# A transformer block on one core: its early transfers relaid and put in another order

## The chip, the core and the metric

The kernel runs on one core of one Trainium2 chip. The metric is device time in microseconds (us) from start to end of one execution. The engines are called PE (TensorE), DVE (VectorE), ACT (ScalarE), POOL (GpSimd) and SP (SyncE, which here only issues DMAs). They run side by side, each through its own instructions in order, and wait for one another through semaphores. 16 DMA engines move data from HBM to the core's memory (SBUF).

## What is computed

`x` is 1024 tokens by 256. A conditioning vector `c` gives six modulation vectors (shift, scale and gate, for the attention part and for the feed-forward part). The block is:

```python
mod = (silu(c) @ wmod).reshape(1, 6, 1, 256)
sa, ca, ga, sb, cb, gb = (mod[:, i] for i in range(6))
ga = (2 * (ga >= 0) - 1) * maximum(abs(ga), 0.25)      # gb likewise
h = layernorm(x) * (1 + ca) + sa
x = x + ga * attention(h)      # 64 latents, compressed to 32, norm, q k v, rotary, causal softmax
h = layernorm(x) * (1 + cb) + sb
x = x + gb * ffn(h)            # 2048 hidden; gate, up and down weights in 4 bits with a scale per 32
```

## The kernel before, in words

Everything is resident in SBUF. The 1024 tokens are 8 tiles of 128, worked on in two halves of 4 tiles (h = 0, 1). The feed-forward weights come in 8 groups of 256 hidden units; ACT, DVE and POOL decode a group while PE multiplies with an earlier one. The order on each engine is written out by hand, and there is no scheduler. Each row of code is one instruction or a short run of them in that order.

The order of the transfers is the order in which SP issues them (L306 to L315): the first half of `x`, `consts` (an identity of 128x128 first, then two selection matrices, two masks and four columns), the columns of `wmod` for shift and scale of the attention part, the second half of `x`, the other four of the six vectors' columns of `wmod` (1024 KB), the rotary table `rope`, and then for each group g its `packed` bits and its `scales`. ACT issues four small ones beside them (L326 to L329: `c`, two packs of small attention weights of 168 and 20 KB, the output bias). Both queues feed the same 16 DMA engines. `scales` has 8 rows per group, each spread over 16 partitions.

The beginning runs as one chain through several engines:

- DVE takes the statistics of the first half of `x` (`stats1(0)`, L553 to L560, waits for `x_in[0]`). POOL adds two weights (L514, waits for `a64_in`) and then makes the reciprocal root (`rsqrt`, L501). DVE normalises (L570).
- PE first multiplies a tile of zeros 14 times (`stay_warm`, a helper that only keeps PE busy), then with the small weights (waits for `a64_in`, `wsum_ready`), 3 more times zeros, transposes the normalised half (`transpose1(0)`, L891, against the identity), makes shift and scale (`mod_columns`, waits for `wmod_in[0]`), and compresses (`project_c(0)`).
- Then PE waits for `wmod_in[1]` and makes the gate `ga` (`products(bank(GA_B, D), ...)`), multiplies zeros 4 times, and turns the compressed half around (`transpose_c(0)`, L930, waits for `chat_ready`, which DVE gives at L599). With that, DVE's `gamma_beta(0)`, PE's `project_qkv(0)`, DVE's `rotate(0)` (waits for `rope_in`) and PE's `stack_qk(0)` follow one from another.

Every small instruction of PE is recorded at L866, the helper `mm`. The lines on which the order of PE's beginning rests are these:

```python
            project_c(0)
            pe.wait_ge(wmod_in[1], 16)
            products(bank(GA_B, D), [(silu[:, k:k + 1].to_broadcast([P, P]), wmod_sb[:, k, GA * D:(GA + 1) * D])
                                   for k in range(KT)]).then_inc(ga_done, 1)
            stay_warm(3, 4)
            transpose_c(0)
```

Of the kernel before, what the change touches and what calls it, by code (L numbers as in the profile page):

```python
# [27 lines left out]
P = 128  # L28
T, D = 1024, 256
DLAT, DC = 64, 32  # L30
FF = 2048
TILES = T // P
HALF = 512
HT = HALF // P
# [15 lines left out]
C_ID, C_SELQ, C_SELK, C_MASK, C_MASKT, C_QM = 0, P, 2 * P, 3 * P, 4 * P, 5 * P  # L50
# [20 lines left out]
def build_block(nc, x, wmod, c_col, attn64, attn32, b_out, consts, rope, packed, scales, out):  # L71
    with ExitStack() as ctx:  # L72
# [13 lines left out]
        xres = sb("xres", [P, TILES, D])  # L86
        wmod_sb = sb("wmod_sb", [P, KT, 6 * D])
# [58 lines left out]
        wmod_flat = wmod_sb[:].rearrange("p k n -> p (k n)")  # L146
# [5 lines left out]
        ident = cst[:, C_ID:C_ID + P]  # L152

        x_in = [sem("x_in0"), sem("x_in1")]
        c_in, a64_in, a32_in, cst_in, bout_in, rope_in = sem("c_in"), sem("a64_in"), sem("a32_in"), sem("cst_in"), sem("bout_in"), sem("rope_in")
# [74 lines left out]
        x_d = x[0].rearrange("(i p) d -> p i d", p=P)  # L230
        out_d = out[0].rearrange("(i p) d -> p i d", p=P)
        wmod_d = wmod.rearrange("(k p) n -> p k n", p=P)
# [71 lines left out]
        @block.sync  # L304
        def _(sp):
            sp.dma_start(xres[:, 0:HT, :], x_d[:, 0:HT, :]).then_inc(x_in[0], 16)  # L306
            sp.dma_start(cst[:], consts).then_inc(cst_in, 16)
            sp.dma_start(wmod_sb[:, :, 0:2 * D], wmod_d[:, :, 0:2 * D]).then_inc(wmod_in[0], 16)
            sp.dma_start(xres[:, HT:, :], x_d[:, HT:, :]).then_inc(x_in[1], 16)
            sp.dma_start(wmod_sb[:, :, 2 * D:], wmod_d[:, :, 2 * D:]).then_inc(wmod_in[1], 16)  # L310
            sp.dma_start(rope_sb[:], rope).then_inc(rope_in, 16)
            for g in range(GROUPS):
                sp.dma_start(wbuf[:, g, 0, :].bitcast(I32), packed[g]).then_inc(bits_in[g], 16)

                sp.dma_start(wbuf[:, g, 1, :],  # L315
                             scales[g].unsqueeze(1).to_broadcast([P // REP, REP, WORDS])
                             ).then_inc(scale_in[g], 16)
# [223 lines left out]
        def _(dve):  # L541
# [81 lines left out]
            def split_qk(h):  # L623

                dst = (QS[0:QK, h, :], KS[0:QK, HALF * h:HALF * (h + 1)])
# [238 lines left out]
        def _(pe):  # L864
# [8 lines left out]

            def mod_columns(o, vec, paired):
                for k in range(KT):
                    base = vec * D + (k if paired else k * P)
                    step = 2 if paired else 1
                    for kt in range(KT):
                        last = mm(o[:, k:k + 1], wmod_sb[:, kt, base:base + step * (P - 1) + 1:step],
                                  silu[:, kt:kt + 1], kt == 0, kt == KT - 1)  # L880
                return last

            def transpose1(h):
                pe.wait_ge(cst_in, 16)
# [58 lines left out]
            def stack_qk(h):  # L943

                pe.wait_ge(prod_ready, h + 1)
# [117 lines left out]
            products(bank(GA_B, D), [(silu[:, k:k + 1].to_broadcast([P, P]), wmod_sb[:, k, GA * D:(GA + 1) * D])  # L1063
# [32 lines left out]
            products(bank(3, D), [(silu[:, k:k + 1].to_broadcast([P, P]), wmod_sb[:, k, GB * D:(GB + 1) * D])  # L1096
# [101 lines left out]
```

## Time and profile before

| what | value |
|---|---|
| time, median of 3 runs | 216.76 us (214.21 to 218.32) |
| time of the profiled execution | 217.49 us |
| its span, first to last instruction | 215.5 us |
| mean granted clock of PE | 0.949 |
| busy: PE, DVE, ACT, POOL | 198.3, 142.7, 90.8, 59.4 us |
| bytes read from HBM | 10.09 MB |
| SP waits, longest | 123.4 us for DVE, before it stores the first output |

The profile is of one execution. The span does not hold what lies around the first and the last instruction, about 2 us here. The granted clock is the share of full speed that the chip's throttle left to PE: 1.0 is 2.4 GHz, 0.5 is 1.2 GHz.

### The profile page before, as it was taken

How to read it: one execution, taken by the hardware profiler on the slowest of the kernel's cores; microseconds unless marked ns; L12 is line 12 of the kernel's file. 1: busy time of each engine (PE TensorE's matmuls, PEld its weight loads, DVE VectorE, ACT ScalarE, POOL GpSimd, SP SyncE). 2: the span in 40 equal slices, each digit the busy share in tenths (PEclk: the TensorE clock that was granted, in tenths of full speed). 3: DMA queues.
4: the chain of work that ended last, by engine and by line, in shares of the span. 5: the costliest groups of instructions: out<-in, count | busy, mean ns of one | idle time of the engine just before them, and what ended most of it. 6: DMA issues, size and time to landing. Idle time of an engine off the chain costs nothing. (4 is left out here: it accounts for less than half of the span.)

```text
span 215.5 us, 3087 instructions
## 1 busy us (share of the span) xinstructions
PE 198.3 (92%) x1064; PEld 159.3 (74%) x1064; DVE 142.7 (66%) x267; ACT 90.8 (42%) x151; POOL 59.4 (28%) x52
## 2 busy tenths in 40 slices
PE   7899998999769969989999999999899999999991
PEld 2496476574446848878898889887698889889891
DVE  0665995878799999999999844945832333323235
ACT  2011141642478526437535556354243542552420
POOL 4404043515152620200000000463342633624200
PEclk9885895599999999999999999999999999999998
DMA  5999675400000000000000000000200000000002
GB/s 177 324 349 235 193 230 196 171 4 3 0 0 2 0 0 3 2 0 0 3 0 0 3 0 0 0 0 5 97 2 0 0 0 0 3 0 0 0 0 97
DMA packets 5644, 11.30 MB, mean 52 GB/s; under 512 B 544, under 2 KB 2752, under 8 KB 5632
## 3 DMA queue, kind: packets, MB, share of 16 engines
q1 hardware_dynamic: 5216, 10.82, 16.0%
q10 hardware_dynamic: 416, 0.33, 0.6%
q8 instruction: 7, 0.11, 0.2%
q14 instruction: 5, 0.04, 0.1%
HBM read 10.09 MB, written 1.05 MB: 52 GB/s over the span
## 5 line engine op out<-in xcount | busy, mean ns | idle before, releaser
L866 PE MATMUL ps<-H,WS 128*128 128x512 f32 x384 | 94.7, 394 | 3.6 <-DVE wmod_sb L714 2.8
L866 PEld LDWEIGHTS ps<-H,WS 128*128 128x128 f32 x384 | 69.6, 188 | 18.9 <-DVE wmod_sb L714 4.3
L866 PEld LDWEIGHTS ps<-WS,IS 128*128 128x128 f32 x384 | 49.8, 191 | 3.8 <-issue 1.7
L866 PE MATMUL ps<-WS,IS 128*128 128x256 f32 x384 | 50.9, 283 | 1.1 <-DVE wmod_sb L714 0.9
L429 ACT ACTIVATE IS<-wmod_sb 128x512 fp32r<-128x512 f32 x32 | 20.3, 634 | 64.1 <-PE ps L866 41.0
L284 DVE TENSOR_TENSOR IS<-wmod_sb,IS 128x512 fp32r<-128x512 f32 x32 | 22.1, 690 | 26.6 <-ACT IS L429 25.0
L293 POOL TENSOR_TENSOR WS<-wbuf,WS 128x1024 fp32r<-128x1024 f32 x10 | 24.2, 2421 | 50.3 <-ACT WS L410 50.3
L714 DVE TENSOR_TENSOR wmod_sb<-ps,wmod_sb 128x512 f32<-128x512 f32 x32 | 22.0, 688 | 22.7 <-PE ps L866 20.7
L298 POOL TENSOR_TENSOR WS<-wbuf,WS 128x512 fp32r<-128x512 f32 x10 | 13.7, 1371 | 38.4 <-ACT WS L417 38.4
L423 ACT ACTIVATE wmod_sb<-ps 128x512 f32<-128x512 f32 x32 | 18.7, 586 | 6.2 <-PE ps L866 6.2
L866 PE MATMUL ps<-idle 128*128 128x512 bf16 x46 | 16.3, 502 | 1.3 <-POOL idle L487 1.3
L410 ACT ACTIVATE WS<-wbuf 128x1024 fp32r<-128x1024 f32 (+1 forms) x16 | 16.8, 1051 | 0.0
L501 POOL TENSOR_TENSOR rstd<-var,power 128x4 f32<-128x4 f32 x6 | 7.2, 1202 | 34.2 <-DVE var L560 27.2
L866 PEld LDWEIGHTS ps<-idle 128*128 128x128 bf16 x46 | 5.2, 122 | 8.5 <-issue 5.4
L866 PE MATMUL ps<-PH,VS 128*128 128x512 f32 (+3 forms) x24 | 8.9, 402 | 2.7 <-DVE PL L258 2.1
L696 DVE SCALAR_TENSOR_TENSOR wbuf<-dec_b,wbuf 128x768 f32<-128x768 f16 x8 | 10.9, 1366 | 0.1
L417 ACT ACTIVATE WS<-wbuf 128x512 fp32r<-128x512 f32 (+1 forms) x16 | 9.9, 618 | 0.0
L553 DVE BATCH_NORM_STATS2 stats<-xres 128x6 f32<-128x256 f32 x16 | 5.6, 415 | 5.0 <-DMA xres<-x 5.0
L401 ACT ACTIVATE dec_a<-wbuf 128x768 int32<-128x768 uint8 x8 | 6.7, 838 | 4.8 <-DMA wbuf<-packed 4.8
L687 DVE SCALAR_TENSOR_TENSOR dec_b<-dec_a,dec_b 128x768 int32<-128x768 int32 x8 | 8.3, 1042 | 0.1
L866 PEld LDWEIGHTS ps<-PH,VS 128*128 128x128 f32 x24 | 4.8, 206 | 4.4 <-ACT PH L368 4.0
L509 POOL TENSOR_TENSOR xres<-xres,gab 128x256 f32<-128x256 f32 x8 | 6.1, 792 | 7.0 <-DVE gab L776 7.0
(116 smaller groups left out, 203.3 us busy)
## 6 DMA issues: line engine op xcount, KB each, us to landing
wbuf<-packed SPq DMA_DIRECT2D x8, 384.0 KB, 17.7
wbuf<-scales SPq DMA_DIRECT2D x8, 384.0 KB
xres<-x SPq DMA_DIRECT2D x2, 512.0 KB, 6.2
wmod_sb<-wmod SPq DMA_DIRECT2D x1, 1024.0 KB, 11.0
out<-xres SPq DMA_DIRECT2D x4, 256.0 KB, 2.2
wmod_sb<-wmod SPq DMA_DIRECT2D x1, 512.0 KB, 7.1
rope_sb<-rope SPq DMA_DIRECT2D x1, 512.0 KB, 12.0
cst<-consts SPq DMA_DIRECT2D x1, 322.0 KB, 5.3
```

Of the source, the lines that this page charges most:

```text
L284: engine.tensor_tensor(IS[:, b, 1, :], inter[:, b, :], IS[:, b, 0, :].bitcast(F32), ALU.subtract).then_inc(i_lo, 1)
L293: engine.tensor_tensor(WS[:, par, 1, :, 0:2, :], wgroup(g)[:, :, 0:2, :], WS[:, par, 0, :, 0:2, :].bitcast(F32), ALU.subtract).then_inc(wg ...
L298: engine.tensor_tensor(WS[:, par, 1, :, 2, :], wgroup(g)[:, :, 2, :], WS[:, par, 0, :, 2, :].bitcast(F32), ALU.subtract).then_inc(wd_lo, 1)
L410: act.activation(WS[:, par, 0, :, 0:2, :], src[:, :, 0:2, :], ACT.Copy).then_inc(wgu_hi, 1)
L417: act.activation(WS[:, par, 0, :, 2, :], src[:, :, 2, :], ACT.Copy).then_inc(wd_hi, 1)
L423: act.activation(gel[:, b, :], bank(unit_banks(n)[0]), ACT.Gelu_apprx_tanh).then_inc(gelu_done, 1)
L429: act.activation(IS[:, b, 0, :], inter[:, b, :], ACT.Copy).then_inc(i_hi, 1)
L501: pool.tensor_tensor(rstd[:, k, :], var[:, k, :], power[:], ALU.pow).then_inc(rstd_ready[k], 1)
L687: dve.scalar_tensor_tensor(dec_b[:], dec_a[:, g % 2, :], MAGNITUDE, dec_b[:], ALU.bitwise_and, ALU.bitwise_or).then_inc(spread_used, 1)
L696: dve.scalar_tensor_tensor(wbuf[:, g, 1, :], vals[:, :, 1], FP16_BIAS, wbuf[:, g, 1, :], ALU.mult, ALU.mult).then_inc(dec_done, 1)
L714: dve.tensor_tensor(inter[:, b, :], bank(unit_banks(n)[1]), gel[:, b, :], ALU.mult).then_inc(inter_done, 1)
L866: return pe.matmul(o, lhsT, rhs, start=start, stop=stop)
```

## The change

`x` is rearranged on the host, so that each partition's 8 rows of 256 numbers lie one behind another, and the identity of 128x128, which was in `consts`, is put in front of them. The first transfer thus brings the identity and the first half of `x` in one run of 4608 bytes per partition (before: 4 runs of 1024). `wmod` is rearranged too: the columns of vectors 0 and 1 of both halves in one run of 4096 bytes per partition (before 2 of 2048), those of vectors 2 to 5 in one of 8192 (before 2 of 4096). The transfers' order is new: the first half of `x`, `wmod` 0 and 1, the second half of `x`, `consts`, then for group 0 the first half of `rope` and the group's bits and scales, then the second half of `rope`, the rest of `wmod` (`wmod_in[1]`), and group 1. The waits follow: the transposes wait for `x_in[0]` rather than `cst_in`, and `stack_qk` and `split_qk` wait for `cst_in` themselves. No compute instruction is added or taken away.

```diff
-            sp.dma_start(xres[:, 0:HT, :], x_d[:, 0:HT, :]).then_inc(x_in[0], 16)
+            first = P + HT * D
+            sp.dma_start(head[:, 0:first], x[:, 0:first]).then_inc(x_in[0], 16)
+            sp.dma_start(wmod_flat[:, 0:KT * 2 * D], wmod[:, 0:KT * 2 * D]).then_inc(wmod_in[0], 16)
+            sp.dma_start(head[:, first:], x[:, first:]).then_inc(x_in[1], 16)
             sp.dma_start(cst[:], consts).then_inc(cst_in, 16)
-            sp.dma_start(wmod_sb[:, :, 0:2 * D], wmod_d[:, :, 0:2 * D]).then_inc(wmod_in[0], 16)
-            sp.dma_start(xres[:, HT:, :], x_d[:, HT:, :]).then_inc(x_in[1], 16)
-            sp.dma_start(wmod_sb[:, :, 2 * D:], wmod_d[:, :, 2 * D:]).then_inc(wmod_in[1], 16)
-            sp.dma_start(rope_sb[:], rope).then_inc(rope_in, 16)
             for g in range(GROUPS):
+                if g < 2:
+                    sp.dma_start(rope_sb[:, HALF * g:HALF * (g + 1)], rope[:, HALF * g:HALF * (g + 1)]
+                                 ).then_inc(rope_in[g], 16)
+                if g == 1:
+                    sp.dma_start(wmod_flat[:, KT * 2 * D:], wmod[:, KT * 2 * D:]).then_inc(wmod_in[1], 16)
                 sp.dma_start(wbuf[:, g, 0, :].bitcast(I32), packed[g]).then_inc(bits_in[g], 16)
...
-                dve.wait_ge(rope_in, 16)
+                dve.wait_ge(rope_in[h], 16)
...
             def split_qk(h):
 
+                dve.wait_ge(cst_in, 16)
...
             def transpose1(h):
-                pe.wait_ge(cst_in, 16)
+                pe.wait_ge(x_in[0], 16)
...
             def stack_qk(h):
 
+                pe.wait_ge(cst_in, 16)
                 pe.wait_ge(prod_ready, h + 1)
...
-    consts[:, C_ID:C_ID + P] = eye
+    x = np.concatenate([eye, a["L0_attn_x"].reshape(TILES, P, D).transpose(1, 0, 2).reshape(P, TILES * D)], 1)
+    wmod = a["L0_wmod"].reshape(KT, P, 6, D).transpose(1, 0, 2, 3)
+    wmod = np.concatenate([wmod[:, :, 0:2].reshape(P, -1), wmod[:, :, 2:].reshape(P, -1)], 1)
```

On SP the first DMAs of the program stand in this order in the kernel before (`128x4x256` is partitions by runs by elements):

```order
L306 DMA xres<-x 128x4x256
L307 DMA cst<-consts 128x644
L308 DMA wmod_sb<-wmod 128x2x512
L309 DMA xres<-x 128x4x256
L310 DMA wmod_sb<-wmod 128x2x1024
L311 DMA rope_sb<-rope 128x1024
L313 DMA wbuf<-packed 128x768
L315 DMA wbuf<-scales 128x1x768
L313 DMA wbuf<-packed 128x768
```

and in this order in the changed kernel, where `head` holds the identity and `x`:

```order
L307 DMA head<-x 128x1152
L308 DMA wmod_flat<-wmod 128x1024
L309 DMA head<-x 128x1024
L310 DMA cst<-consts 128x516
L313 DMA rope_sb<-rope 128x512
L317 DMA wbuf<-packed 128x768
L319 DMA wbuf<-scales 128x1x768
L313 DMA rope_sb<-rope 128x512
L316 DMA wmod_flat<-wmod 128x2048
L317 DMA wbuf<-packed 128x768
```

The 1024 KB transfer of `wmod` has moved from the fifth place to the ninth, behind `rope` and the bits and scales of group 0.

On PE the instructions around the gate `ga` stand so before, with the semaphores that each waits for:

```order
L866 MATMUL ps<-wcm,xnT 128x32 [waits t1_ready,wcm_ready]
L866 MATMUL ps<-wcm,xnT 128x32 x7
L866 MATMUL ps<-wmod_sb,silu 128x256 [waits wmod_in1]
L866 MATMUL ps<-wmod_sb,silu 128x256
L866 MATMUL ps<-idle 128x512 x4
L930 MATMUL ps<-cst,csq 32x128 [waits chat_ready]
```

and so in the changed kernel:

```order
L871 MATMUL ps<-wcm,xnT 128x32 [waits t1_ready,wcm_ready]
L871 MATMUL ps<-wcm,xnT 128x32 x7
L871 MATMUL ps<-wmod_flat,silu 128x256 [waits wmod_in1]
L871 MATMUL ps<-wmod_flat,silu 128x256
L871 MATMUL ps<-idle 128x512 x4
L940 MATMUL ps<-head,csq 32x128 [waits chat_ready]
```

Nothing has moved on PE: the gate's products still stand between `project_c(0)` and `transpose_c(0)` and still wait for `wmod_in1`; only the transfer behind that semaphore comes at another place in SP's order.

## Rows read from the trace of the kernel before

**Rows 1.** The page: PE busy, granted clock, DMA share, GB/s, 40 slices of 5.4 us.

```profile
PE   7899998999769969989999999999899999999991
PEclk9885895599999999999999999999999999999998
DMA  5999675400000000000000000000200000000002
GB/s 177 324 349 235 193 230 196 171 4 3 0 0 2 0 0 3 2 0 0 3 0 0 3 0 0 0 0 5 97 2 0 0 0 0 3 0 0 0 0 97
```

**Rows 2.** Chain that ended last, in order of time: start us, us, what.

```profile
154.71 55.42 PE ps L866 x324
```

**Rows 3.** Timeline of PE: start us, us, instruction [idle before it <-what ended it].

```profile
7.34 0.63 PE L866 MATMUL ps<-a 64*128 64x32 f32 x4 [0.73 <-DMA a<-attn]
8.21 0.70 PE L866 MATMUL ps<-wsum,a 64*128 64x256 f32 x2 [0.25 <-POOL wsum L514]
...
14.62 2.53 PE L866 MATMUL ps<-wcm,xnT 128*128 128x32 f32 x16
16.96 2.05 PE L866 MATMUL ps<-wmod_sb,silu 128*128 128x256 f32 x4
18.80 1.91 PE L866 MATMUL ps<-idle 128*128 128x512 bf16 x4
20.51 1.06 PE L930 MATMUL ps<-cst,csq 128*32 128x128 f32 x4
```

**Rows 4.** Timeline of SP: start and length of DMA issues (L306, L310, L313 twice).

```profile
0.74 0.44 SPq L306 DMA_DIRECT2D xres<-x  x1
...
2.75 0.88 SPq L310 DMA_DIRECT2D wmod_sb<-wmod  x1
...
4.25 0.46 SPq L313 DMA_DIRECT2D wbuf<-packed  x1
...
5.54 0.41 SPq L313 DMA_DIRECT2D wbuf<-packed  x1
```

**Rows 5.** The tiles xres and wmod_sb: landing of L306, then of L310.

```profile
DMA to landing us min/median/max: 4.3/4.3/4.3
...
DMA to landing us min/median/max: 11.0/11.0/11.0
```

**Rows 6.** The tile wbuf: landing of L313 for group 0, then for group 1.

```profile
DMA to landing us min/median/max: 13.1/13.1/13.1
...
DMA to landing us min/median/max: 16.7/16.7/16.7
```

**Rows 7.** Windows: us, length, busy of five engines, PEclk, DMA share, GB/s.

```profile
1.50:3.50 2.00, 2.00 (x6) 0.68 (x5) 0.00 (x0) 0.60 (x1) 1.62 (x5) 1.00 0.37 108
5.50:7.25 1.75, 1.11 (x5) 0.32 (x3) 1.65 (x10) 0.00 (x0) 0.00 (x0) 1.00 1.04 236
8.50:9.25 0.75, 0.75 (x4) 0.26 (x4) 0.07 (x1) 0.00 (x0) 0.75 (x2) 0.84 1.07 345
9.50:12.50 3.00, 3.00 (x15) 2.72 (x14) 2.19 (x8) 0.59 (x1) 0.35 (x1) 0.51 1.01 396
...
14.75:18.00 3.25, 3.25 (x20) 3.07 (x20) 2.44 (x13) 0.68 (x1) 1.01 (x1) 0.67 1.08 214
...
22.50:26.00 3.50, 3.50 (x14) 2.01 (x14) 3.32 (x7) 0.49 (x1) 0.00 (x0) 0.98 0.53 171
33.00:43.00 10.00, 8.80 (x34) 6.09 (x33) 6.67 (x13) 4.04 (x10) 4.92 (x5) 0.50 0.48 183
```

**Rows 8.** Timeline of DVE and POOL: start us, us, instruction [idle before it].

```profile
5.04 1.41 DVE L553 BATCH_NORM_STATS2 stats<-xres 128x6 f32<-128x256 f32 x4 [5.04 <-DMA xres<-x]
...
7.44 0.72 POOL L514 TENSOR_TENSOR wsum<-a 64x256 f32<-64x256 f32 x1 [4.08 <-DMA a<-attn]
8.12 1.02 POOL L501 TENSOR_TENSOR rstd<-var,power 128x4 f32<-128x4 f32 x1
...
9.18 1.46 DVE L570 TENSOR_SCALAR xn<-xres,mv,rstd 128x256 f32<-128x256 f32 x4 [1.65 <-POOL rstd L501]
...
19.75 0.29 DVE L599 TENSOR_TENSOR csq<-cc,rstd 128x128 f32<-128x128 f32 x1
```

More of the change, by code:

```diff
@@ L46 @@
 MAGNITUDE, SIGN = 0x0E000E00, 0x10001000
-C_ID, C_SELQ, C_SELK, C_MASK, C_MASKT, C_QM = 0, P, 2 * P, 3 * P, 4 * P, 5 * P
+C_SELQ, C_SELK, C_MASK, C_MASKT, C_QM = 0, P, 2 * P, 3 * P, 4 * P
 C_KM, C_OM, C_WM, C_N = C_QM + 1, C_QM + 2, C_QM + 3, C_QM + 4
@@ L84, in build_block @@
         GATE, UP, Y = 0, 1, 2
-        xres = sb("xres", [P, TILES, D])
-        wmod_sb = sb("wmod_sb", [P, KT, 6 * D])
+        head = sb("head", [P, P + TILES * D])
+        ident = head[:, 0:P]
+        xres = head[:, P:].rearrange("p (i d) -> p i d", i=TILES)
+        wmod_flat = sb("wmod_flat", [P, KT * 6 * D])
+        wmod_a = wmod_flat[:, 0:KT * 2 * D].rearrange("p (k n) -> p k n", k=KT)
+        wmod_b = wmod_flat[:, KT * 2 * D:].rearrange("p (k n) -> p k n", k=KT)
         c_sb = sb("c_sb", [P, KT])
@@ L144, in build_block @@
         WS = sb("WS", [P, 2, 2, 2, 3, 2 * P], F32R)
-        wmod_flat = wmod_sb[:].rearrange("p k n -> p (k n)")
         gel = wmod_flat[:, 0:2 * HALF].rearrange("p (b n) -> p b n", b=2)
@@ L150, in build_block @@
         IS = sb("IS", [P, 2, 2, HALF], F32R)
-        ident = cst[:, C_ID:C_ID + P]
         x_in = [sem("x_in0"), sem("x_in1")]
-        c_in, a64_in, a32_in, cst_in, bout_in, rope_in = sem("c_in"), sem("a64_in"), sem("a32_in"), sem("cst_in"), sem("bout_in"), sem("rope_in")
+        c_in, a64_in, a32_in, cst_in, bout_in = sem("c_in"), sem("a64_in"), sem("a32_in"), sem("cst_in"), sem("bout_in")
+        rope_in = [sem("rope_in0"), sem("rope_in1")]
         wmod_in = [sem("wmod_in0"), sem("wmod_in1")]
@@ L228, in build_block @@
         ys_ready, y_ready = sem("ys_ready"), sem("y_ready")
-        x_d = x[0].rearrange("(i p) d -> p i d", p=P)
         out_d = out[0].rearrange("(i p) d -> p i d", p=P)
-        wmod_d = wmod.rearrange("(k p) n -> p k n", p=P)
         def bank(b, n=512, p0=0, p1=P):
@@ L872, in products, with mod_weights @@
                 return last
+            def mod_weights(vec):
+                return (wmod_a, vec) if vec < GA else (wmod_b, vec - 2)
             def mod_columns(o, vec, paired):
+                w, vec = mod_weights(vec)
                 for k in range(KT):
@@ L878, in mod_columns @@
                     for kt in range(KT):
-                        last = mm(o[:, k:k + 1], wmod_sb[:, kt, base:base + step * (P - 1) + 1:step],
+                        last = mm(o[:, k:k + 1], w[:, kt, base:base + step * (P - 1) + 1:step],
                                   silu[:, kt:kt + 1], kt == 0, kt == KT - 1)
@@ L1062, in _ @@
             pe.wait_ge(wmod_in[1], 16)
-            products(bank(GA_B, D), [(silu[:, k:k + 1].to_broadcast([P, P]), wmod_sb[:, k, GA * D:(GA + 1) * D])
+            products(bank(GA_B, D), [(silu[:, k:k + 1].to_broadcast([P, P]), wmod_b[:, k, (GA - 2) * D:(GA - 1) * D])
                                    for k in range(KT)]).then_inc(ga_done, 1)
@@ L1095, in _ @@
             pe.wait_ge(x1_ready, HT)
-            products(bank(3, D), [(silu[:, k:k + 1].to_broadcast([P, P]), wmod_sb[:, k, GB * D:(GB + 1) * D])
+            products(bank(3, D), [(silu[:, k:k + 1].to_broadcast([P, P]), wmod_b[:, k, (GB - 2) * D:(GB - 1) * D])
                                   for k in range(KT)]).then_inc(gb_done, 1)
@@ L1186 @@
     arrays = {
-        "x": a["L0_attn_x"], "wmod": a["L0_wmod"],
+        "x": x, "wmod": wmod,
         "c_col": np.ascontiguousarray(a["L0_c"].reshape(KT, P).T),
```

## Prediction

> **What bounds the kernel now.** I read the page first, then the chain that ended last, the timelines of PE, SP, DVE and POOL for the first 29 us, the landing times of single transfers, and windows of the first 45 us. On the page PE is busy in nearly every slice, and the DMA engines work only in the first eight and for a moment at the outputs [rows 1]. The chain that ended last is PE's from 154.71 us on [rows 2]: the end is set by how early PE gets through all its work. No transfer that this change touches is awaited after the first 20 us. So the change can act only by moving the beginning, and whatever shift PE has at `transpose_c(0)` is carried to the end, because from there each step waits for the one before it (PE, DVE, PE, DVE) and neither PE nor DVE has a free stretch to take it up.
>
> The beginning in rows: the first half of `x` is there at 5.04, and DVE starts [rows 8]. POOL waits until 7.44 for the small attention weights, adds them, and only then makes the root, at 8.12; the normalised `x` follows at 9.18 [rows 8]. PE runs out of its zeros, waits 0.73 for the same weights and a further 0.24 (from 7.34 + 0.63 to 8.21) for POOL's sum [rows 3]. Then it is in work without a pause: compression at 14.62, the gate's products at 16.96, zeros at 18.80, `transpose_c(0)` at 20.51 [rows 3]. What `transpose_c(0)` needs from DVE starts at 19.75 and takes 0.29, so it is there at 20.04 [rows 8]: of the two, PE itself is the later, by 0.5.
>
> The gate's weights were issued at 2.75 and took 11.0 [rows 4, 5]: landed at 13.75, 3.2 us before PE used them. That is all the slack there is in moving them back.
>
> **The change, part by part.**
>
> *Longer runs for the first half of `x`.* Before: issued at 0.74, landed 4.3 later [rows 4, 5]. Between 1.5 and 3.5 us the DMA engines were 0.37 busy at 108 GB/s, though work was queued [rows 7]; the 512 short rows come to the engines slowly. The new transfer is 590 KB in 128 rows. At 396 GB/s, which rows of 4 KB reach from 9.5 to 12.5 [rows 7], it takes 1.5; from a start near 1.9 and with about 0.7 until the last part is reported, it lands near 4.2. That is 0.8 earlier; bounds 0 (the engines start as slowly as before) and 1.4.
>
> The Trainium skill, page "DMA: Bandwidth & Descriptors", section "Specifications", gives 512 bytes and more as enough for line rate. By that rule the rows of 1024 bytes lost nothing and relaying brings nothing. The rows differ from it a little: 345 GB/s while the second half of `x` moves in rows of 1 KB, against 396 [rows 7]. By the rule the arrival of the gate's weights below would be later by the 1.5 that I take off, and the sum larger by as much.
>
> *The rest of the head.* Rows of 2 KB (`wmod` 0 and 1, with the ACT queue's weights between) moved at 236 GB/s [rows 7]. At 396 its 524 KB take 1.3 rather than 2.2, 0.9 less; the second half of `x` 0.2 less. I take 0.7 of these 1.1. `consts` comes later, but the identity is now in front, and its other users stand at 22 us and later. The extra waits for `cst_in` and the tenth DMA issue find their semaphore set and cost nothing; if `consts` were not there, `stack_qk` would wait, yet it is the fourth of SP's transfers.
>
> *What PE gains before the gate.* The small weights land earlier by about the same 0.8 to 1.5, which is enough to be there when the first 14 zeros end. PE's waits of 0.73 and 0.24 go [rows 3]; POOL's root then comes 1 us or more earlier and does not hold the transposes. Gain 0.9 (bounds 0 and 1.0, since the zeros themselves end at 6.6). PE is then ready for the gate at 16.96 − 0.9 = 16.05.
>
> *When the gate's weights come now.* Ahead of them are now `rope` first half (262 KB), `packed` 0 (393 KB), `scales` 0 (393 KB) and `rope` second half (262 KB). At 396 GB/s the two halves of `rope` take 1.32 and `packed` 0.99. `scales` is the unknown one. At 396 it would also take 0.99: sum 3.3, the lower bound. But `packed` of group 0 was issued at 4.25 and took 13.1, landing at 17.35, that of group 1 was issued at 5.54 and took 16.7, landing at 22.24 [rows 4, 6]: 4.9 us for the `scales` and the `packed` between, of which 0.99 are `packed` at best. So `scales` took up to 3.9, and the throughput in that time fell to 214 GB/s at full DMA share [rows 7]. I take 3.5, near the upper end, because this is the very transfer. Sum 1.32 + 0.99 + 3.5 = 5.8. Arrival: 13.75 + 5.8 − 0.8 (head start) − 0.7 (longer rows) = 18.05, say 18.0. Lower end: 13.75 + 3.3 − 1.4 − 1.1 = 14.6. Upper end: 13.75 + 6.2 = 20.0.
>
> Why so slow? From 33 to 43 us, with nothing but groups in the queue, the DMA share is 0.48 [rows 7]: half the engines stand idle. The Trainium skill, same page, section "Rules for kernel authors" ("Use all 16 engines"), says that an outermost dimension smaller than 16 keeps a transfer on at most so many engines; `scales` has 8. The trace agrees with the 0.48. By that rule alone `scales` would take 2.0 (half of 396 GB/s); that is between my ends, and it is the first rival below.
>
> *What then waits.* PE is ready at 16.05 and stands until 18.0: a new wait of about 2 us at the gate. Queued behind it on PE are the 4 zeros and `transpose_c(0)`; for that DVE's `gamma_beta(0)` waits, and for it all of q, k and v. The products start 18.0 − 16.96 = 1.04 later than before, and from there to `transpose_c(0)` it is 3.55 as before (16.96 to 20.51 [rows 3]). DVE's part would have been ready about 19.1, so nothing hides it.
>
> *What comes earlier and is free.* The bits of group 0 land earlier than 17.3, but ACT's decoding feeds DVE only at 22 us. The bits and scales of group 1 keep their place in the total of bytes, and the later groups too; SP's list is only one DMA longer.
>
> **Sum.** −0.9 at PE's start, +1.95 of wait at the gate: +1.04. On the profiled execution's time, 217.49, this is 218.5. The median of the runs shown is 216.76, 0.7 less than that execution, so against the median 217.8.
>
> **Rivals.**
>
> *The weights arrive in time* (0.28). With half of the DMA engines at work (the share of 0.48) but each at its full rate, `scales` takes 393 KB at 198 GB/s, 2.0, and the weights land at 13.75 + 1.32 + 0.99 + 2.0 − 1.5 = 16.6: 0.4 sooner than PE used them before, so 216.4. With the head's upper values (2.5 for 1.5) as well they land before 16.05, and the whole 0.9 is kept. For it: the DMA engines had a poor start, 108 GB/s, and `scales` now meets less else in the queue. Against it: 4.9 us between the landings of the two `packed`. Time: 216.76 − 0.9 = 215.9 to 216.4.
>
> *The clock comes back later* (0.10, slower). The granted clock is at half, the 1.2 GHz level, in the fourth slice [rows 1], and back at 0.98 from 22.5 to 26 with PE 3.5 of 3.5 busy [rows 7]. A PE that stands for 2 us and then starts late could find it at the 1.2 GHz level for that stretch too. Price: 3.5 more for the same work, 1.0 + 3.4 = 4.4, so 221.2. It decides from about 221.1.
>
> *The clock's later stretch at half goes* (0.10, faster). From 33 to 43 us PE was granted 0.50 with 8.80 busy [rows 7]; at the 2.4 GHz level that is up to 4.4 less. If the shift keeps it at the upper level, and the weights are in time, 216.76 − 0.9 − 4.4 = 211.5. Nothing in the trace says that a shift of 1 us does this, nor that it does not; DVE would also have to keep up.
>
> *The late gate as summed* (0.52): 217.8.
>
> **Numbers.** Likeliest is the late gate, 217.8; its own range is 216.8 to 219.2 (arrivals from 17.0 to 19.4). The runs shown spread by 1.9% on their own, so 2% is about what a measurement of this kernel can tell from no change. The range goes from 214.8 (the case in time, less 1.1 of the spread) to 220.0 (weights at 20.0, +3.0 on 216.76) and leaves out the two clock cases. Faster by over 2% (below 212.4) is the one clock case, 0.10; slower by over 2% (above 221.1) the other, 0.10; within 2% 0.80.
>
> **What would show it.** In the profile after: the first half of `x` lands near 4.2; no PE wait, or a short one, at the small weights; L316 lands near 18, issued near 4.8, so 13 us to landing; PE idle about 2 us ahead of the gate's products; `transpose_c(0)` at 21.5. If L316 lands before 16, the price of `scales` was wrong and the rival in time holds. If it lands at 18 and the time is still below that of before, then the shift is not carried, and I have misread the chain from `transpose_c(0)` on.

## The result and the profile after

The changed kernel takes 221.59 us (median of 4, 220.83 to 223.12), the kernel before beside it 216.7: 1.0274 times as long, 95% interval 1.0162 to 1.0386. In a second set of six it took 221.97 against 217.63, ratio 1.0168 (1.0108 to 1.0227). It is slower, by 4 to 5 us in the medians, and lies above the forecast range (214.8 to 220.0). The profiled execution took 221.13 us with a span of 219.1. The ratios leave out the slowest executions of either kernel, which the means further down do not.

The page's rows that answer to [rows 1]:

```profile
PE   7797989799768977989999999999799999999991
PEclk9875878569999999999999999999999999999998
DMA  6999765300000000000000000000110000000002
GB/s 207 318 278 305 220 214 189 116 0 3 0 0 1 0 0 3 1 0 0 3 0 0 0 3 0 0 0 4 58 39 0 3 0 0 0 0 0 0 0 96
```

PE is as full as before. The granted clock has one more dip, in the sixth slice (27.4 to 32.9 us), and the long dip behind it comes a slice later. The timeline of PE, to be read against [rows 3] (start us, us, instruction [idle before it <- what ended it]):

```profile
8.00 0.63 PE L871 MATMUL ps<-a 64*128 64x32 f32 x4 [1.02 <-DMA a<-attn]
8.87 0.70 PE L871 MATMUL ps<-wsum,a 64*128 64x256 f32 x2 [0.24 <-POOL wsum L518]
...
10.53 1.91 PE L901 MATMUL ps<-head,xn 128*128 128x128 f32 x8
...
15.28 2.46 PE L871 MATMUL ps<-wcm,xnT 128*128 128x32 f32 x16
18.89 2.08 PE L871 MATMUL ps<-wmod_flat,silu 128*128 128x256 f32 x4 [1.15 <-DMA wmod_flat<-wmod]
20.75 1.91 PE L871 MATMUL ps<-idle 128*128 128x512 bf16 x4
22.46 1.06 PE L940 MATMUL ps<-head,csq 128*32 128x128 f32 x4
...
26.57 3.51 PE L871 MATMUL ps<-prod,cst 128*128 128x512 f32 x4 [0.22 <-DVE prod L620]
...
32.28 0.33 PE L871 MATMUL ps<-KS,QS 96*128 96x128 f32 x1 [0.76 <-DVE KS L633]
```

The gate's products are the row that reads `wmod_flat,silu 128x256`. They start at 18.89, not 16.96, and PE stood 1.15 before them, for the transfer. But PE was late before that already: it waited 1.02 for the small weights and began with them at 8.00, 0.66 later than before, and the transposes at 10.53 are 0.57 later. `transpose_c(0)` comes at 22.46, 1.95 later. The two products of `stack_qk(0)`, four instructions in the trace, take 3.51 at 26.57. These are three rows of the kernel before that answer to them and were not shown above:

```profile
9.96 1.91 PE L891 MATMUL ps<-cst,xn 128*128 128x128 f32 x8
...
24.66 1.98 PE L866 MATMUL ps<-prod,cst 128*128 128x512 f32 x4
...
28.77 0.33 PE L866 MATMUL ps<-KS,QS 96*128 96x128 f32 x1 [0.38 <-DVE KS L628]
```

So 1.95 us of lateness became 1.91 at `stack_qk(0)`, and 3.51 at the first score (28.77 to 32.28); 3.6 is the difference of the spans. The 1.5 us in between come with the clock. Windows from 26.8 to 30.2 us (length, busy of PE, PEld, DVE, ACT, POOL, granted clock, DMA share, GB/s), before:

```profile
26.80:30.20 3.40, 2.92 (x21) 2.17 (x21) 3.12 (x7) 2.67 (x5) 2.71 (x4) 1.00 0.79 229
```

and after:

```profile
26.80:30.20 3.40, 3.40 (x6) 1.27 (x6) 2.02 (x5) 0.16 (x2) 1.67 (x3) 0.50 0.75 217
```

In this stretch PE was granted the full clock before and half of it, the 1.2 GHz level, after. The 3.51 us of `stack_qk(0)` fall into it.

The transfers: issues of the first half of `x` and of the gate's weights on SP, of the small weights on ACT, and then the time from issue to landing of each, in that order.

```profile
0.73 0.40 SPq L307 DMA_DIRECT2D head<-x  x1
...
5.22 0.44 SPq L316 DMA_DIRECT2D wmod_flat<-wmod  x1
...
1.18 0.52 ACTq L331 DMA_DIRECT2D a<-attn  x1
```

```profile
DMA to landing us min/median/max: 3.9/3.9/3.9
...
DMA to landing us min/median/max: 13.6/13.6/13.6
...
DMA to landing us min/median/max: 6.8/6.8/6.8
```

They land at 4.6 (DVE starts on the first half of `x` at 4.66; forecast 4.2), 18.8 (forecast 18.0) and 8.0. The small weights of the kernel before took

```profile
DMA to landing us min/median/max: 6.1/6.1/6.1
```

from 1.22, that is 7.3. The new beginning of the list did not bring them forward: they came 0.7 later.

### The profile page after: what moved, and what is told of

It is laid out like the page before. It is cut to its first block and busy times, and to the rows that moved or that the text cites. A ratio compares the mean times of both kernels' runs of the same rounds, so it can differ in the third digit from the quotient of the medians.

```text
span 219.1 us, 3092 instructions
## 1 busy us (share of the span) xinstructions
PE 199.8 (91%) x1064; PEld 160.0 (73%) x1064; DVE 142.3 (65%) x267; ACT 90.5 (41%) x151; POOL 59.4 (27%) x52
## 3 DMA queue, kind: packets, MB, share of 16 engines
HBM read 10.09 MB, written 1.05 MB: 51 GB/s over the span
## 5 line engine op out<-in xcount | busy, mean ns | idle before, releaser
L433 ACT ACTIVATE IS<-wmod_flat 128x512 fp32r<-128x512 f32 x32 | 20.2, 632 | 64.2 <-PE ps L871 41.1
L284 DVE TENSOR_TENSOR IS<-wmod_flat,IS 128x512 fp32r<-128x512 f32 x32 | 22.1, 691 | 26.5 <-ACT IS L433 25.0
L719 DVE TENSOR_TENSOR wmod_flat<-ps,wmod_flat 128x512 f32<-128x512 f32 x32 | 22.0, 688 | 22.8 <-PE ps L871 20.8
L427 ACT ACTIVATE wmod_flat<-ps 128x512 f32<-128x512 f32 x32 | 18.7, 584 | 6.2 <-PE ps L871 6.2
L557 DVE BATCH_NORM_STATS2 stats<-head 128x6 f32<-128x256 f32 x16 | 5.6, 412 | 4.7 <-DMA head<-x 4.7
L513 POOL TENSOR_TENSOR head<-head,gab 128x256 f32<-128x256 f32 x8 | 6.1, 789 | 8.2 <-DVE gab L781 8.2
L371 ACT ACTIVATE PF<-ps 128x512 f32<-128x512 f32 (+3 forms) x12 | 6.0, 497 | 4.6 <-PE ps L871 4.6
## 6 DMA issues: line engine op xcount, KB each, us to landing
wbuf<-packed SPq DMA_DIRECT2D x8, 384.0 KB, 17.1
```

The costliest lines, as they stand in the source:

```text
L284: engine.tensor_tensor(IS[:, b, 1, :], inter[:, b, :], IS[:, b, 0, :].bitcast(F32), ALU.subtract).then_inc(i_lo, 1)
L427: act.activation(gel[:, b, :], bank(unit_banks(n)[0]), ACT.Gelu_apprx_tanh).then_inc(gelu_done, 1)
L433: act.activation(IS[:, b, 0, :], inter[:, b, :], ACT.Copy).then_inc(i_hi, 1)
L719: dve.tensor_tensor(inter[:, b, :], bank(unit_banks(n)[1]), gel[:, b, :], ALU.mult).then_inc(inter_done, 1)
```

## Two things to read in every execution

Each execution has a time and a mean granted clock. The clock has two levels here, 1.0 and 0.5, so from the two numbers follows the time that PE spent at half clock: 2 x (1 - 0.943) x 219.1 = 25.0 us for the profiled one. Over all 227 executions of this study that came with a clock, with a level of its own for each kernel, a us more at half clock makes an execution 0.43 us longer (standard error 0.01). The table has the means over all executions that came with a clock.

| kernel | executions | mean us | mean us at half clock |
|---|---|---|---|
| before | 87 | 217.2 | 20.4 |
| changed (first set and g2) | 10 | 221.8 | 27.8 |
| e1, order back | 4 | 221.4 | 27.0 |
| e2, order alone | 4 | 220.7 | 23.2 |
| e4, 4 zeros ahead of the gate | 4 | 221.1 | 26.9 |
| e5, before and 5 zeros | 4 | 216.4 | 16.5 |
| f1, 4 zeros at the start | 12 | 220.6 | 23.6 |
| f2, small weights first | 6 | 223.0 | 30.1 |
| f3, layout alone, small weights first | 12 | 218.4 | 23.6 |
| f4, scales over 16 engines | 6 | 222.5 | 30.3 |
| g1, 5 zeros ahead of the gate | 6 | 220.5 | 24.0 |
| g3, before, small weights late | 6 | 222.5 | 28.6 |
| g4, f3 and 5 zeros | 12 | 220.4 | 24.1 |
| h1, zeros in both places | 6 | 219.4 | 19.5 |
| h2, layout, all early | 12 | 218.6 | 24.9 |
| h3, before, small weights early | 12 | 217.6 | 22.0 |
| h4, changed, small weights early | 6 | 221.6 | 27.8 |
| i1, h2 and 4 zeros | 12 | 218.6 | 21.9 |
| i2, h2 and 8 zeros | 6 | 218.2 | 17.1 |

The loss of the changed kernel, 221.8 - 217.2 = 4.6, is thus 7.4 x 0.43 = 3.2 of clock and 1.4 (standard error 0.2) of lateness at equal clock. This is an observed relation and not yet a cause; e4, f1, g1 and h1 test whether it can be acted on.

## Experiments

### Which late arrival

*e1: the gate's weights back in their old place, the layout kept.*

```diff
             sp.dma_start(cst[:], consts).then_inc(cst_in, 16)
+            sp.dma_start(wmod_flat[:, KT * 2 * D:], wmod[:, KT * 2 * D:]).then_inc(wmod_in[1], 16)
...
-                if g == 1:
-                    sp.dma_start(wmod_flat[:, KT * 2 * D:], wmod[:, KT * 2 * D:]).then_inc(wmod_in[1], 16)
```

> The changed kernel with the rest of wmod issued right behind consts again, ahead of rope and group 0; the new layout stays. Theory late gate (PE's shift comes from the gate's weights landing at 18.8 instead of 13.75): the weights land near 13, PE does not wait at the gate, the gate's products start about 17.6 (16.96 and the 0.66 that the small weights came later), transpose_c(0) near 21.2, time 217.4. Rival new runs (the long rows in front cost the time, through the small weights and whatever else they push back): the time stays at 220 or above. Rival head only: the 0.66 is all that is left, and it is carried to the end.

Measured: 221.14 against 217.87, ratio 1.0219 (1.0002 to 1.0436). Its timeline of PE:

```profile
7.79 0.63 PE L870 MATMUL ps<-a 64*128 64x32 f32 x4 [0.45 <-DMA a<-attn]
...
10.20 1.75 PE L900 MATMUL ps<-head,xn 128*128 128x128 f32 x8
11.73 3.41 PE L870 MATMUL ps<-silu,wmod_flat 128*128 128x1 f32 x16
...
16.27 3.60 PE L870 MATMUL ps<-wcm,xnT 128*128 128x32 f32 x16
19.69 2.05 PE L870 MATMUL ps<-wmod_flat,silu 128*128 128x256 f32 x4
```

No wait at the gate, and yet its products start at 19.69. The shift and scale columns (`128x1`) take 3.41 here, 2.29 in the profile of the changed kernel, and the compression 3.60, not 2.46: they ran at half clock. The expectation of 17.6 and 217.4 fell. The late gate is not enough to explain the loss, since without it most of the loss stays: 3.9 in the means against the kernel before beside it, 1.3 (standard error 0.4) at equal clock.

*e2: the kernel before, only the gate's weights moved back.*

```diff
-            sp.dma_start(wmod_sb[:, :, 2 * D:], wmod_d[:, :, 2 * D:]).then_inc(wmod_in[1], 16)
...
             for g in range(GROUPS):
+                if g == 1:
+                    sp.dma_start(wmod_sb[:, :, 2 * D:], wmod_d[:, :, 2 * D:]).then_inc(wmod_in[1], 16)
```

> The kernel before with its layout untouched, and only the 1024 KB of wmod moved behind group 0's packed and scales (rope is still whole and ahead). Theory late gate: the weights land near 19 to 20, PE idles 2 to 3 us before the gate's products, time 219.5 to 221.5, most of what the whole change cost. Rival new runs: no more than 0.5 above the kernel before, 217.2.

Measured: 220.77 against 217.87, ratio 1.0218 (1.0045 to 1.0391). PE's compression and the gate's products:

```profile
13.44 3.50 PE L867 MATMUL ps<-wcm,xnT 128*128 128x32 f32 x16
20.96 2.07 PE L867 MATMUL ps<-wmod_sb,silu 128*128 128x256 f32 x4 [4.02 <-DMA wmod_sb<-wmod]
```

A stand of 4.0 us and 220.8: the order alone costs about 3 us as well (2.2 at equal clock). So each of the two alone costs most of the whole, and together they do not cost the sum. They lie beside each other: PE reaches the gate late for one reason, and the weights arrive late for the other.

*h4: the changed kernel, small weights issued by SP behind the first half of `x`.*

```diff
-            act.dma_start(a64[:], attn64).then_inc(a64_in, 16)
...
             sp.dma_start(head[:, 0:first], x[:, 0:first]).then_inc(x_in[0], 16)
+            sp.dma_start(a64[:], attn64).then_inc(a64_in, 16)
```

> The changed kernel with its order, and only the small weights moved to SP right behind the first half of x. Theory late gate: PE reaches the gate about 1 us sooner and stands there about 3 us, because the weights land near 19 all the same; the start gained nothing, 221.5 or more. Rival that the small weights were the larger cause: 219 or below.

Measured: median 221.48 against 217.74; these executions spread too far for an interval.

```profile
9.13 1.31 PE L901 MATMUL ps<-head,xn 128*128 128x128 f32 x8 [0.47 <-DVE xn L574]
...
12.87 3.62 PE L871 MATMUL ps<-wcm,xnT 128*128 128x32 f32 x16
19.60 2.08 PE L871 MATMUL ps<-wmod_flat,silu 128*128 128x256 f32 x4 [3.11 <-DMA wmod_flat<-wmod]
```

PE begins the transposes at 9.13, 1.4 earlier than in the changed kernel, gets through the compression by 16.5 and then stands 3.11 for the gate's weights. Nothing of the gain is left, as the late gate predicts.

*f2: the changed kernel, small weights ahead of `c` on ACT's queue.*

```diff
-            act.dma_start(c_sb[:], c_col).then_inc(c_in, 16)
             act.dma_start(a64[:], attn64).then_inc(a64_in, 16)
+            act.dma_start(c_sb[:], c_col).then_inc(c_in, 16)
```

> The changed kernel with ACT's first two issues exchanged: the small attention weights (168 KB) before c. Theory that the new runs push the small weights back and the rest follows from it: they land near 6 instead of 7.95, PE's wait of 1.02 goes, the transposes start about 1 us sooner (9.6), less time at half clock, 219.5. Rival late gate: PE then just waits 1 us longer at the gate (2.1 instead of 1.15), whose weights land at 18.8 all the same, and the time stays at 221.5.

Measured: 221.74 against 216.51, ratio 1.0224 (1.0142 to 1.0305). Small weights at 5.7, transposes at 9.05, a wait of 1.44 at the gate, no gain: the rival holds.

*g3: the kernel before, the bias ahead of the small weights on ACT's queue.*

```diff
             act.dma_start(c_sb[:], c_col).then_inc(c_in, 16)
+            act.dma_start(bout_sb[:], b_out.unsqueeze(0).to_broadcast([P, D])).then_inc(bout_in, 16)
             act.dma_start(a64[:], attn64).then_inc(a64_in, 16)
             act.dma_start(a32[:], attn32).then_inc(a32_in, 16)
-            act.dma_start(bout_sb[:], b_out.unsqueeze(0).to_broadcast([P, D])).then_inc(bout_in, 16)
```

> The kernel before with the bias issued ahead of the two packs of small weights on ACT's queue: they land about 1 us later, as in the changed kernel, and nothing else is altered. Theory that the late small weights are a cause: PE waits 1.5 instead of 0.7 for them, the transposes start 0.7 later, and 218 to 219.5 comes out, the upper value if the longer stand costs clock too. Rival gate only: within 0.3 of the kernel before plus nothing, 217.

Measured: 222.1 against 217.63, ratio 1.0201 (1.0142 to 1.0261).

```profile
10.14 1.06 PE L866 MATMUL ps<-a 64*128 64x32 f32 x4 [3.50 <-DMA a<-attn]
...
13.42 1.91 PE L891 MATMUL ps<-cst,xn 128*128 128x128 f32 x8
```

The dose came out larger than meant: the weights landed at 10.1, not 8.3, and the transposes 3.5 later than before. The 3.5 us of lateness cost 222.5 - 217.3 = 5.2 in the means (217.3 is the kernel before beside it), of which 1.7 (standard error 0.3) at equal clock and the rest with 8 us more at half. This does not show how much the 0.7 of the changed kernel cost.

### Is the layout worth anything

*f3: small weights first on ACT and the gate's weights back (f2 and e1 together). h2: the same with the small weights on SP, so that `c` stays first. h3: the kernel before with only the small weights on SP.*

```diff
             sp.dma_start(xres[:, 0:HT, :], x_d[:, 0:HT, :]).then_inc(x_in[0], 16)
+            sp.dma_start(a64[:], attn64).then_inc(a64_in, 16)
```

(h3; h2 is this line behind `head`, with e1's edit)

> The changed kernel with the small weights first on ACT and the rest of wmod back ahead of rope and group 0: of the change only the layout stays. Theory that the loss is made of the two late arrivals (small weights and gate's weights): both are gone, 216 to 217, a little under the kernel before. Rival that the long runs themselves cost something else: it stays above 219.

> Layout of the change, small weights issued by SP right behind the first half of x, c first on ACT as in both kernels, gate's weights ahead of rope and group 0. Theory of the two late arrivals plus the clock: small weights land near 5.3, c by 4.8, transposes at 8.8 (before 9.96), nothing waits at the gate; 1.1 us less than the kernel before at equal clock, 215.5 to 216.5. Rival that the long runs bring nothing in the end: 217 to 218.

> The kernel before with one thing altered: the small weights issued by SP right behind the first half of x. Theory that their arrival is what counts at the start and the layout little: they land near 6, the transposes start 0.6 to 0.9 earlier, 216.5 or a little less. If h2 is below this by 0.5 or more, the long runs are worth that.

Measured: f3 219.52 against 216.51, ratio 0.9983 (0.9912 to 1.0054); h2 217.85 against 217.74, 0.9944 (0.9885 to 1.0004); h3 217.75 against 217.74, 1.001 (0.9965 to 1.0055). For f3 the median and the ratio do not agree in sign. In the means f3 lies 1.6 above the kernel before beside it, h2 0.9 above and h3 equal, so none of the three forecasts of 215.5 to 217 was reached. With both arrivals early the loss is gone but for the clock: at equal time at half clock f3 lies 0.2 below the kernel before, h3 0.4 and h2 0.6 (standard error 0.2 each). This row of DVE in f3 shows what its exchange cost, a wait for ACT's exponential of `c`, which now landed late:

```profile
8.26 0.17 DVE L739 TENSOR_SCALAR silu_t<-silu_t 128x2 f32<-128x2 f32 x1 [1.50 <-ACT silu_t L336]
```

In h2, with `c` first, that wait is gone:

```profile
9.20 1.31 PE L900 MATMUL ps<-head,xn 128*128 128x128 f32 x8
...
15.41 2.05 PE L870 MATMUL ps<-wmod_flat,silu 128*128 128x256 f32 x4
```

The transposes are 0.8 earlier than in the kernel before and the gate's products 1.5 (16.96 to 15.41), and still its median is equal: its executions hold 24.9 us at half clock against 20.4, with three of twelve at 34 to 35. So the long runs are not shown to be worth anything (h2 against h3, 0.2 at equal clock, standard error 0.3), and no version with them is shown to be faster than the kernel before.

*f4: the changed kernel with each of the 8 rows of scales stored 16 times.*

```diff
-                             scales[g].unsqueeze(1).to_broadcast([P // REP, REP, WORDS])
+                             scales[g]
...
+    scales = np.repeat(scales, REP, 1)
```

> The changed kernel with the scales stored 16 times on the host, so that each partition has a row of its own and the transfer runs over all DMA engines; the order stays. Theory scales on 8 engines is what makes the gate's weights late: they land near 15.5 instead of 18.8 and PE does not wait for them; what is left is the small weights: 219.5 to 220. Rival late order: three times as many bytes from HBM or not, landing stays at 18 or later, 221.5.

Measured: 222.32 against 216.51, ratio 1.0283 (1.0222 to 1.0345). Windows of f4, from 11 to 14.5 and from 33 to 40 us:

```profile
11.00:14.50 3.50, 3.50 (x19) 3.50 (x18) 1.41 (x5) 1.33 (x2) 0.45 (x2) 0.50 1.05 431
33.00:40.00 7.00, 7.00 (x39) 6.63 (x38) 3.75 (x12) 0.00 (x0) 0.23 (x1) 0.58 0.00 0
```

and of the changed kernel:

```profile
11.00:14.50 3.50, 3.50 (x23) 3.45 (x21) 1.52 (x5) 1.33 (x2) 0.15 (x1) 0.69 1.07 247
33.00:40.00 7.00, 6.32 (x45) 5.43 (x44) 4.91 (x13) 0.59 (x1) 1.47 (x1) 0.79 0.52 189
```

431 GB/s rather than 247 while group 0 and the gate's weights move, and no DMA at all after 33 us, where the changed kernel's DMA engines are still busy for 0.52. Both pages give 10.09 MB read from HBM, so the bytes moved are the same. The gate's weights, issued at 4.91, took

```profile
DMA to landing us min/median/max: 11.2/11.2/11.2
```

and landed at 16.1. The price of `scales` was read rightly: it is their spreading, 8 rows over 16 partitions each. But the time did not follow. The gate's products in that execution:

```profile
20.07 2.06 PE L871 MATMUL ps<-wmod_flat,silu 128*128 128x256 f32 x4
```

PE reached the gate at 20.07, at half clock since 10.2, and had not waited for the weights. The expected 219.5 to 220 did not come: in this execution taking the transfer off the path gained nothing, because the clock already held PE back, and all six executions had 29 to 32 us at half clock.

### The clock

*g2: the changed kernel again.*

> The changed kernel once more, unaltered, beside the others on one chip, because the share of the clock in the loss rests on four executions. Theory that most of the loss is the clock: its executions hold 25 to 31 us at half clock, those of the kernel before 16 to 22, and the times follow by about 0.45 us for each us. Rival: with more executions the two overlap in time at half clock, and a loss of 4 to 5 us stays at equal clock.

Measured: 221.97 against 217.63, ratio 1.0168 (1.0108 to 1.0227), 22 to 35 us at half clock. Of its profiled execution, PE and the landing of the gate's weights (issued at 5.07):

```profile
8.01 0.63 PE L871 MATMUL ps<-a 64*128 64x32 f32 x4 [0.70 <-DMA a<-attn]
...
10.42 1.92 PE L901 MATMUL ps<-head,xn 128*128 128x128 f32 x8
12.13 3.41 PE L871 MATMUL ps<-silu,wmod_flat 128*128 128x1 f32 x16
...
16.67 3.60 PE L871 MATMUL ps<-wcm,xnT 128*128 128x32 f32 x16
20.08 2.05 PE L871 MATMUL ps<-wmod_flat,silu 128*128 128x256 f32 x4
...
23.64 0.83 PE L940 MATMUL ps<-head,csq 128*32 128x128 f32 x4
```

```profile
DMA to landing us min/median/max: 14.0/14.0/14.0
```

The weights were there at 19.1, PE came at 20.08. The same kernel that stood 1.15 us at the gate in one execution did not wait in the other. What had changed is where the half clock fell: the shift and scale columns took 3.41, not 2.29. The first expectation holds for the means (27.8 against 20.4 us at half, and 1.4 left at equal clock, not 4 to 5). Single executions of the two kernels do overlap in time at half clock: 22 to 35 and 13 to 35 us.

*e4 and g1: zeros ahead of the wait for the gate's weights, 4 taken from behind the products (e4) or 5 additional ones (g1). f1: 18 instead of 14 zeros at the start. h1: f1 and g1 together.*

```diff
-            stay_warm(WC_B, 14)
+            stay_warm(WC_B, 18)
...
             project_c(0)
+            stay_warm(3, 5)
             pe.wait_ge(wmod_in[1], 16)
```

> The changed kernel with the 4 multiplications of zeros ahead of the wait for the gate's weights instead of behind the gate's products. Theory late gate with the wait carried: zeros from 17.7 to 19.6 fill the wait, the gate's products start 19.5 and transpose_c(0) near 21.5 rather than 22.46, about 1 us less: 220.5. If PE's idling (1.15 us) is also what put the clock to half at 26.8, that stretch is gone and another 1.5 us: 219. Rival that the shift is not what counts: no change, 221.6.

> The changed kernel with 5 more multiplications of zeros ahead of the wait for the gate's weights, the 4 behind the products kept. They fill the time in which PE stood (1.15 us, and the rest at half clock), and delay nothing much, since the weights land at 18.8 anyway. Theory clock by idling (PE's stand before the gate brings 6 us more at half clock): time at half clock from 28 to about 20 us, time 218.5. Theory late start alone: 221.5 or 0.5 more.

> The changed kernel with 18 instead of 14 multiplications of zeros at the start, so that PE does not stand still from 6.6 to 8.0 while the small weights come. No work of the block starts earlier by it. Theory idle PE costs through the clock (the time at half clock, 25 to 31 us in the changed kernel's executions against 18 to 22 before, is what makes half of the loss): time at half clock falls to about 21 us, time 219.3. Theory late start alone (lateness is carried, the clock is luck): no change, 221.6, or 0.3 slower.

> The changed kernel with zeros in both places where PE stood: 18 instead of 14 at the start and 5 more ahead of the wait for the gate's weights. No work of the block is earlier. Each alone took the mean time at half clock from 28 to 24 us. Theory clock by idling: together about 20 us as in the kernel before, and with 0.45 per us and the lateness of 2 us kept, 219. Rival (the length of the beginning, not the idling, sets the clock): 24 us again and 220.7.

Measured: e4 220.91 against 217.87, ratio 1.02 (0.9936 to 1.0464), not to be told from the changed kernel; g1 221.32 against 217.63, 1.0144 (1.0083 to 1.0205); f1 220.93 against 216.51, 1.0042 (0.9962 to 1.0123) with a mean of 220.6; h1 218.89 against 217.74, 1.0132 (1.0066 to 1.0198). g1 (24.0 us at half) and f1 (23.6) fell short of their forecasts of about 20 and 21 us and of 218.5 and 219.3. In the profile of e4 the wait at the gate is gone and the first score starts at 29.34, 2.9 earlier than in the changed kernel, yet this execution took 223.56. Its window from 33 to 54 us, where the changed kernel's clock was 0.76, shows why:

```profile
33.00:54.00 21.00, 19.59 (x66) 13.99 (x67) 11.50 (x26) 6.74 (x14) 7.66 (x7) 0.51 0.28 99
```

What the beginning gains, a later stretch at half clock can take again, and nothing here shows what decides that. The timeline of PE in h1:

```profile
8.00 0.63 PE L871 MATMUL ps<-a 64*128 64x32 f32 x4
...
10.41 1.47 PE L901 MATMUL ps<-head,xn 128*128 128x128 f32 x8
...
18.51 1.91 PE L871 MATMUL ps<-idle 128*128 128x512 bf16 x4 [0.22 <-issue]
20.22 1.15 PE L871 MATMUL ps<-wmod_flat,silu 128*128 128x256 f32 x4
...
22.07 0.60 PE L940 MATMUL ps<-head,csq 128*32 128x128 f32 x4
```

In h1 no piece of the block's work is started earlier by the edit; PE only multiplies zeros where it stood. Its transposes are as late as in the changed kernel (10.41), and its executions hold 19.5 us at half clock instead of 27.8 (difference 8.3, standard error 1.5) and take 219.4 in the mean instead of 221.8 (difference 2.4, standard error 0.7). The forecast of 219 for it, from 0.45 us per us at half clock, held. That makes the clock a cause and not a companion: filling both stands gave back 2.4 us. What remains, 2.2 us above the kernel before with no more time at half clock, is lateness: 2.6 at equal clock, of which the zeros themselves brought 1.2. Each filling alone took about 4 us of half clock, and gained 1.2 and 1.3, which is not clear of the error (0.8 each).

*e5: the kernel before with 9 instead of 4 zeros behind the gate's products.*

```diff
-            stay_warm(3, 4)
+            stay_warm(3, 9)
             transpose_c(0)
```

> The kernel before with 9 instead of 4 multiplications of zeros behind the gate's products: PE never idles there, but transpose_c(0) is 5 x 0.43 = 2.1 us later. Theory that a shift at transpose_c(0) is carried one to one and idling costs through the clock: 218.8, with no stretch at half clock between 24 and 31 us. Theory that the shift itself brings the clock back to half at 26.8 (other work falls into the time that decides): 220.3 or more. Rival that something downstream takes a shift up: under 217.7.

Measured: 216.18 against 217.87, ratio 1.0022 (0.9867 to 1.0177). The forecast of 218.8 was missed; the time is the one named for "something downstream takes a shift up". A deliberate delay of PE cost nothing that can be seen, with 16.5 us at half clock, the lowest mean of all 19 kernels. At equal clock it lies 0.9 (standard error 0.4) above the kernel before, about what 5 zeros take at full clock (5 x 0.21). So the numbers fit a delay that is carried and a clock that pays for it, but that the zeros bought the clock is not shown. Four executions are few, and in the profiled one a part of the gain lies ahead of them. The zeros run at 17.63, and the clock was full here already from 9.5 to 12.5, where the kernel before had 0.51 [rows 7]:

```profile
9.50:12.50 3.00, 2.94 (x24) 2.59 (x24) 2.18 (x7) 0.60 (x1) 0.17 (x1) 1.00 1.05 422
```

*g4, i1 and i2: can it be bought in the kernels with both arrivals early? g4 is f3 with e5's edit. i1 is h2 with 4 zeros ahead of `project_c(1)`, i2 has 4 more behind `max_rows(0)`.*

```diff
             last.then_inc(modb_done, 1)
+            stay_warm(4, 4)
             project_c(1)
             max_rows(0)
+            stay_warm(4, 4)
```

> Layout of the change, small weights first, gate's weights ahead of rope and group 0, and 9 instead of 4 multiplications of zeros behind the gate's products. Theory clock by idling: the 5 zeros cost 1.1 us at full clock and save 4 to 7 us at half clock (0.45 each), so 215.5 to 216.5, below both kernels. Rival that zeros there do nothing for the clock: 219.5 and 1 more.

> h2_all_early (long runs, small weights and gate's weights early) with 4 more multiplications of zeros behind the second shift and scale columns, ahead of project_c(1), where PE has only narrow products before the stretch at half clock of 10 to 20 us that starts at 31 to 37 in every run so far. Theory clock by low PE work: the stretch becomes shorter in part of the executions, mean time at half clock from 25 to about 18 us, 3 us gained for 0.9 us of zeros, 216.3 and below the kernel before. Rival (the stretch is set by what follows, not by this place): 0.9 above h2_all_early, 219.

> The same with 4 more zeros behind max_rows(0) too, where PE then waits for ACT anyway. Theory clock by low PE work: another part of the stretch goes, 15 us at half clock, 216 or less. Rival: 1.5 above h2_all_early, 219.5 or more.

Measured: g4 219.55 against 217.63, ratio 1.0086 (1.0046 to 1.0125), half clock 24.1 as in f3: here the same 5 zeros did nothing for it, against the expectation. i1 219.19 against 216.69, 1.0046 (0.9987 to 1.0105), half clock 21.9 against h2's 24.9 (a difference of 3.0, standard error 2.4), mean 218.6 as h2; 216.3 had been expected. i2 218.86 against 216.69 without an interval, half clock 17.1, one execution of six at 6.8 us and 214.15, but the mean 218.2 and not the 216 expected. No version is shown to beat the kernel before. The mean time at half clock is lower with zeros in most places (not in e4 and g4), and the one gain in time that is clear of the error, h1's, came where PE would have stood anyway.

## Why the prediction was wrong, step by step

- **What bounds it.** Right for the profiled execution. PE's chain sets the end, and the shift is carried: 1.95 us at `transpose_c(0)`, 1.91 at `stack_qk(0)`, and nothing is taken up later (3.51 at the first score, 3.6 at the end).
- **Longer runs for `x`.** Mis-sized. The first half was there 0.4 earlier, not 0.8. The stretch from 1.5 to 3.5 us moved 208 GB/s rather than 108 [rows 7], so the mechanism was there, but the transfer brings 64 KB of identity with it. For the start near 1.9 and the 0.7 until the last part is reported, which the forecast of 4.2 used, no row is shown.
- **"What PE gains before the gate".** This is the first step that failed, with the wrong sign. I let the small weights land earlier by 0.8 to 1.5 because the transfer ahead of them ended earlier. They landed 0.7 later. Behind `x` SP now issues 512 KB of `wmod` in the same microsecond, where it had been the 322 KB of `consts`, and both queues share the engines; that this is the reason is argued, and h4 and f2 show only that an earlier issue mends it. So PE was ready for the gate not at 16.05 but at 17.74 (18.89 - 1.15), 0.8 later than before where I had 0.9 earlier, an error of 1.7. In the sum it cancels against the shorter wait, because the gate's products start when their weights land. h4 shows it: PE is ready at 16.5 there, stands 3.11, and nothing is gained.
- **Arrival of the gate's weights.** The mechanism was right and f4 confirms the reason; the size was off by 0.8 (18.8 for 18.0). This is what makes 1.95 out of the sum's 1.04: the products start at 18.89 and `transpose_c(0)` comes at 22.46, for 18.0 and 21.5. The `x` that landed 0.4 and not 0.8 earlier may be half of it; the rest is not measured by itself. The wait itself was 1.15 for 2.0, because PE came late.
- **The clock.** The second step that failed, and the one that decides. The sum has no term for it, and 3.2 of the 4.6 us come that way; at equal clock the change costs 1.4, near the sum's 1.04. I had the mechanism as the slower rival, with 0.10, a price of 3.4 on top and 221.2 in all. That this is near the measured 221.6 is in part luck: the rival's stretch was 22.5 to 26 us, where the clock was granted 0.87 after the change, and the one that fell to half in the profile was 26.8 to 30.2; in g2 it fell elsewhere again. I had treated the clock as one event that either comes or not, where the runs show a time at half clock that differs from execution to execution. The spread of the three runs of the kernel before, 1.9%, which I put down as noise, was probably this: their clocks are not on record, but over 87 executions of that kernel the time at half clock accounts for 0.89 of the variance in time, from 213.60 us with 12.7 at half to 223.22 with 34.5. A change that makes PE stand in two places near a stretch at half clock [rows 7] could lengthen it, and h1, which fills both stands, shows that here it did.
- **The range** ended at 220.0 by adding the upper arrival to nothing of the clock; with the price of the clock case (3.4) on top of that it would have held the time.

What stays open: e1 differs from f3 only in when the small weights and `c` land, and lies 3.0 above it in the means and 1.5 (standard error 0.4) at equal clock, for 0.9 us of difference at the transposes. Four executions of e1 are too few to say whether that is more than the lateness. It is open too why the time at half clock was low with the zeros of e5 and not with those of g4, and why in one kernel the clock falls at other places from execution to execution.

## What to carry to other kernels

When transfers are relaid or reordered, list what is issued by the other queue in the same microseconds and work out its landing as well; a small transfer that shares the engines can be the one that the chain waits for. Moving a transfer back by more than its slack makes the engine stand (here by 5.1 us with a slack of 3.2), and mending one of two late arrivals gained little or nothing while the other held (e1, h4, f2). And when the runs of a kernel spread by 2%, look at their granted clock before calling it noise: where it explains the spread, a new stand of PE can cost clock beside its length. Filling two stands with idle multiplications gave back 2.4 of 4.6 us here.

## What the runs showed of the hardware

- An execution is 0.43 us longer for each us that TensorE spends at half clock; the 19 kernels' own values do not differ from it clearly of the error. PE was busy for 8.80 of 10 us in such a stretch of the kernel before [rows 7]. The same four instructions of `stack_qk(0)` took 1.98 us at a granted clock of 1.00 and 3.51 us mostly at 0.50.
- The clock fell to half while PE was nearly always busy: from 10.2 to 20 us it was granted 0.50 to 0.52 in e1, f4 and g2, with PE busy for 9.5 of 9.8 us. From 7 to 10 us, ahead of it, PE had been busy for 2.0 to 2.3 of 3. In h1, with more zeros at the start, it was busy for 2.75 of those 3, and from 10 to 12 us the clock was still 1.00.
- Single executions of one kernel differ by 20 us and more at half clock (h2, 14.5 to 34.9 us; the kernel before, 12.7 to 34.5), and by 9 to 10 us of time (213.95 to 222.82 and 213.60 to 223.22).
- 8 rows of 3 KB, each spread over 16 partitions, move at 214 to 247 GB/s beside other transfers; the same bytes stored as 128 rows at 431 GB/s. With them the DMA engines had nothing left after 33 us, where those of the changed kernel were still 0.52 busy.
